# The second feed-forward product from fp32r parts, moved behind the projections in odd steps, with its sum behind the cosines

## Chip, cores and metric

One core of one Trainium2 chip. The metric is the device time of one execution in microseconds.

## What is computed

A small attention layer on x (2 x 2048 x 256, 16 heads of 16, full attention, in the reference `_L0_attn_ref`) is followed by two layers of local attention with a gated feed-forward part, with residual sums and normalisations between them. The change lies in the feed-forward part of these two layers:

```python
def _layer(x, wqkv, qs, ksc, wo, lg, lb, w1, b1, w2, b2):
    h = shift_token(x)
    q, k, v = jnp.split(h @ wqkv, 3, axis=-1)
    ...
    x = x + o @ wo
    h = shift_token(x)
    mu = h.mean(-1, keepdims=True)
    var = h.var(-1, keepdims=True)
    h = (h - mu) / jnp.sqrt(var + 1e-05) * lg + lb
    h = h @ w1 + b1
    a, g = jnp.split(h, 2, axis=-1)
    h = a * jax.nn.gelu(g, approximate=False)
    x = x + h @ w2 + b2
    return x
```

h has 682 columns before the last product, x has 256. `shift_token` takes half of the columns from the token before.

## The kernel before

The kernel has three phases. `project_phase` makes q, k and v of the first attention layer. `attention_phase` runs its 32 heads, one after another; beside them it splits the weights of the later phase into fp32r parts (a high part, rounded, and a low part, the rest), piece by piece: SyncE loads a piece (`prepare_weights`), GpSimd rounds and subtracts (`split_piece`), SyncE stores both parts in DRAM. `feed_forward_phase` does the rest; the change is there.

The feed-forward phase handles 64 tiles of 128 tokens (32 of each layer, the two batches in turn) in a software pipeline. Each engine has its own hand-written order, one round of `for t in steps`. In step t an engine works on tile t+3 (transposed x), t+2 (projections, rotary tables, norms), t+1 (local attention), t (normalisation) and on the pair of tiles behind it: in an even step the first product with w1 (`hidden`), GELU (`gelu`, ScalarE) and gate (`gated`, VectorE) of tiles t-2 and t-1; in an odd step the second product with w2 (`hidden_out`, TensorE) of tiles t-3 and t-2, and its sum onto x (`add_hidden`, VectorE). PSUM has eight banks that all these share; most of the waits at the head of a function are for a bank.

The order of an odd step on TensorE is: `scores`, `hidden_out` (line 1358) of tile t-3, `project` (line 1191: three products into three banks, each from fp32r parts), `transposed_probs` (1261), `transposed_hidden_in` (1237), `hidden_out` of tile t-2, `outputs_of_heads` (1303), `transposed_q_k` (1326), `attended` (1342), `transposed_x` (1175).

On VectorE: `mask_and_maximum` (1584) of tile t+1, `split_xT`, the sum `add_hidden` (1615) of tile t-3, `mean_and_variance` (1622) of tile t, which needs x shifted by one token (two DMAs between partitions, from `shift` on SyncE, after the residual sum `add_attended`, 1682, that closes the step before), `normalise` (1598), two `cosines` (1641), `normalise_mid` (1634), `copy_PT` (1655), `square_norms` (1649), `copy_PT`, `rotate` (1662), `scale_keys` (1669), `add_hidden` of tile t-2, `add_attended`.

ScalarE: `exponentials` (1427) of tile t+1, `copy_projected` (1438 to 1441: copy and square of q, copy and square of k, copy of v), `copy_PT` (1448), `affine` (1456), in even steps `gelu`, then `copy_oT`, `copy_qT_kT` (1481, 1483), `round_xT` (1488, 1490). GpSimd: `normalise` (1046), `inverse_deviation` (1051), `add_b2` (1056), `sines` (1067, two instructions; they wait for the copy of k, VectorE's cosines for the squares), `inverse_norms` (1074, 1076), `split_y`, every second step `rotary_tables`.

`hidden_out` takes the gated values `act_T` and w2 as fp32; the projections and `hidden` take fp32r parts, high x high, high x low and low x high, added up in one bank. The pairs of sums and waits that matter:

```python
def normalise_mid(v):
    dve.wait_ge(rstd_made, v + 1)
    if v:
        dve.wait_ge(hT_done, v)
```

Of the kernel before, what the change touches and what calls it, by code (L numbers as in the profile page):

```python
# [6 lines left out]
F32 = mybir.dt.float32  # L7
BF16 = mybir.dt.bfloat16
F32R = mybir.dt.float32r
# [4 lines left out]
P = 128  # L14
# [369 lines left out]
def attention_phase(nc, ins, division, VO, mask_sb, weights, ident, load_output_weights, stacks, qkT_stored):  # L384

    with ExitStack() as ctx:
# [3 lines left out]
        q_stack, k_stack, q_minus_first = stacks.q, stacks.k, stacks.q_minus  # L390
        v_ones = sb("v_ones", [P, BODY, TB, VW])
        probs = sb("probs", [P, PROBS, 512])
        excess = probs[:, PROBS - BLOCKS:].rearrange("p (i k) c -> p i k c", i=2)
        spare_pieces = weights.tables[:].rearrange("p a t h d -> p (a t h d)").rearrange("p (i c) -> p i c", c=PIECE)
        raw_piece, piece_hi, piece_lo = spare_pieces[:, 0], spare_pieces[:, 1].bitcast(F32R), spare_pieces[:, 2].bitcast(F32R)
# [61 lines left out]
        def _(sp):  # L457
# [33 lines left out]
            for n in range(NH):  # L491
# [16 lines left out]
                if n == TABLES_HEAD:  # L508
                    sp.wait_ge(weights.parts_stored, 32 * (len(PIECES) - IN_PLACE))
                    weights.load_tables(sp, ins)  # L510
# [9 lines left out]
        def _(pool):  # L520
# [23 lines left out]
            def split_piece(i):  # L544
# [3 lines left out]
                if i < IN_PLACE:  # L548
                    _, _, k, columns = PIECES[i]
                    hi, lo = weights.wqkv_hi[0][:, k, columns], weights.wqkv_lo[:, k, columns]  # L550
# [154 lines left out]
        def _(dve):  # L705
# [70 lines left out]
          + [("w1", l, k, slice(a, min(a + PIECE, W1_COLUMNS))) for l in range(LAYERS) for k in range(NC) for a in range(0, W1_COLUMNS, PIECE)])  # L776
# [3 lines left out]
class Weights:  # L780


    def __init__(self, nc, ctx, stacks):
# [5 lines left out]
        self.wqkv_hi = [sb("wqkv2_hi0", [P, NC, 3 * INNER], F32R)]  # L789
        self.wqkv_lo = sb("wqkv2_lo", [P, NC, 3 * INNER], F32R)  # L790
        self.tables = sb("tables2", [P, 2, TB, 2, D2 // 2])
# [8 lines left out]
        self.tables_loaded, self.small_loaded = sem("tables2_loaded"), sem("small2_loaded")  # L800
        self.wqkv1_loaded, self.w1_loaded, self.wo_loaded, self.w2_loaded = (sem(n) for n in ("wqkv2_1_loaded", "w1_2_loaded", "wo2_loaded", "w2_loaded"))

    def place_wide(self, ctx, stacks):
# [5 lines left out]
        self.w2 = sb("w2_sb", [P, HC, C])  # L809

    def place_second(self, in_k):

        self.wqkv_hi.append(in_k(NC, 3 * INNER))

    def raw_piece(self, ins, i):
        name, l, k, columns = PIECES[i]
        return ins[name][l].rearrange("(k p) n -> p k n", p=P)[:, k, columns]

    def stored_piece(self, i, part):
        name, l, k, columns = PIECES[i]  # L820
        return self.wqkv_parts[part, :, k, columns] if name == "wqkv2" else self.w1_parts[l, part, :, k, columns]

    def load_tables(self, eng, ins):
        for i, name in enumerate(("cos2", "sin2")):
            eng.dma_start(self.tables[:, i], ins[name].rearrange("(t p) (a d) -> p t a d", p=P, a=2)).then_inc(self.tables_loaded, 16)
# [18 lines left out]
    def load_w2(self, eng, ins, l):  # L844
        eng.dma_start(self.w2[:], ins["w2"][l].rearrange("(k p) n -> p k n", p=P)).then_inc(self.w2_loaded, 16)

    def load_first(self, eng, ins):
# [3 lines left out]
        self.load_w2(eng, ins, 0)  # L851

    def load_second_wqkv(self, eng, part):
        place = (self.wqkv_hi[1], self.wqkv_lo)[part]
        eng.dma_start(place[:].bitcast(F32), self.wqkv_parts[part]).then_inc(self.wqkv1_loaded, 16)


def feed_forward_phase(nc, ins, weights, stacks, division, x_sb, outputs, spare, wo1_loaded, x1_dram, mask_sb, ident, out):

    with ExitStack() as ctx:  # L860
# [17 lines left out]
        weights.place_second(in_k)  # L878
        wqkv_hi, wqkv_lo, (w1_hi, w1_lo), wo_sb, w2_sb = weights.wqkv_hi, weights.wqkv_lo, weights.w1, weights.wo, weights.w2
        qks_sb, cos_sb, sin_sb, b2_sb = weights.qk_scale, weights.tables[:, 0], weights.tables[:, 1], weights.b2  # L880
# [29 lines left out]
        act_T = gate  # L910
# [27 lines left out]
        x1_stored = [sem(f"x1_stored{i}") for i in range(3)]  # L938
        shifted, x1_loaded, out_stored = [sem(f"shifted{i}") for i in range(2)], [sem(f"x1_loaded{i}") for i in range(2)], sem("out_stored")
# [32 lines left out]
        def _(sp):  # L972
# [14 lines left out]
            def shift(v):  # L987
# [5 lines left out]
                if v < 2:  # L993
                    sp.wait_ge(columns_made, 3)
# [9 lines left out]
            weights.load_second_wqkv(sp, 0)  # L1004
            for t in steps:
                if t == 1:
# [895 lines left out]
```

## Time and profile before

| | |
|---|---|
| median of 3 runs | 2899.72 us (2899.66 to 2905.52) |
| the profiled execution | 2905.26 us, of which the span of its instructions is 2903.4 us |
| TensorE busy | 2807.7 us (97%) |
| VectorE busy | 2323.1 us (80%) |
| ScalarE busy | 2113.7 us (73%) |
| GpSimd busy | 960.1 us (33%) |
| second product, line 1358 | 768 records, 195.8 us |
| `normalise_mid`, line 1634 | 64 instructions, 32.7 us |

In the profile PE is TensorE's multiplications, PEld its loads of weights, DVE VectorE, ACT ScalarE, POOL GpSimd, SP SyncE. A share of busy time is a mean over three phases with different limits, so it says little on one step. Instructions of an engine overlap a little in the records: the next often starts some 0.08 to 0.1 us before the one before ends. Times within the span are in us from its start. The feed-forward phase takes the second half of the span; a pair of its steps repeats about every 40.4 us, and tiles 40 and 41 stand for it here. Bank names are left out in the rows, so many operations read `bank<-...`: the line tells them apart.

### The profile page before, as it was taken

To read this page: it belongs to the slowest core of one execution; us is meant where nothing else is said; L and a number is where in the kernel's file an instruction comes from. 1 tells how busy PE (TensorE), PEld (TensorE's weight loads), DVE (VectorE), ACT (ScalarE), POOL (GpSimd) and SP (SyncE) were. 2 spreads that over 40 slices of the span, in tenths; PEclk is the share of its full clock that TensorE was granted. 3 is DMA by queue.
4 is the path that set the end of the run, shared out by engine and by line. 5 is a ranking of instruction groups with operands and counts; after the bars stand their busy time and mean duration, and the time that the engine had idled before them with its cause. 6 is when DMAs were issued, how large, how long until landed. Compare 5 with 4: busy or idle time off the path is not lost. (4 is left out here: it accounts for less than half of the span.)

```text
span 2903.4 us, 59150 instructions
## 1 busy us (share of the span) xinstructions
PE 2807.7 (97%) x22608; PEld 1755.0 (60%) x22608; DVE 2323.1 (80%) x4287; ACT 2113.7 (73%) x4556; POOL 960.1 (33%) x1102
## 2 busy tenths in 40 slices
PE   7999999999999999999997899999999999999997
PEld 7743333333333333333355788888887788888886
DVE  7779999999999999999816677777776677777774
ACT  5568888888888888888856566666666676666763
POOL 7600000010001000000016555555555555656553
PEclk9869999999999999999998899999999999999999
DMA  5613334443444243424203000000000100000000
GB/s 164 189 18 53 52 46 60 62 72 59 70 61 72 55 68 60 74 43 66 42 22 128 11 5 4 5 5 4 5 4 34 54 12 19 19 19 11 20 18 25
DMA packets 85944, 131.33 MB, mean 45 GB/s; under 512 B 33120, under 2 KB 59168, under 8 KB 78240
## 3 DMA queue, kind: packets, MB, share of 16 engines
q1 hardware_dynamic: 79376, 120.41, 21.1%
q10 hardware_dynamic: 6288, 7.14, 0.8%
q8 instruction: 181, 2.97, 0.5%
q14 instruction: 99, 0.81, 0.1%
HBM read 83.98 MB, written 34.61 MB: 41 GB/s over the span
## 5 line engine op out<-in xcount | busy, mean ns | idle before, releaser
L684 ACT ACTIVATE probs<-scores 128x512 f32<-128x512 f32 x2048 | 1114.7, 596 | 199.2 <-PE scores L610 76.3
L717 DVE TENSOR_REDUCE mx<-aux 128x1 f32<-128x1024 f32 x982 | 1201.1, 1223 | 61.4 <-PE aux L578 54.1
L578 PE MATMUL aux<-k_stack,q_stack 48*128 48x512 f32 x2006 | 757.4, 453 | 6.4 <-DMA k_stack<-qk_dram 4.1
L610 PE MATMUL scores<-q_stack,k_stack 50*128 50x512 f32 x2048 | 762.5, 450 | 0.0
L623 PE MATMUL pv<-probs,v_ones 128*32 128x256 f32 x8192 | 658.5, 393 | 0.1
L610 PEld LDWEIGHTS scores<-q_stack,k_stack 50*128 50x128 f32 x2048 | 310.2, 186 | 428.8 <-ACT probs L684 411.2
L623 PEld LDWEIGHTS pv<-probs,v_ones 128*32 128x32 f32 x8192 | 161.7, 108 | 361.5 <-ACT probs L684 289.4
L578 PEld LDWEIGHTS aux<-k_stack,q_stack 48*128 48x128 f32 x2006 | 306.4, 188 | 38.0 <-DVE mx L717 19.2
L531 POOL CAST m_parts<-head_max 128x16 fp32r<-128x16 f32 x32 | 6.3, 198 | 938.6 <-DVE head_max L710 938.6
L1427 ACT ACTIVATE VO<-VO,tables_small 128x256 f32<-128x256 f32 (+1 forms) x512 | 250.9, 492 | 48.7 <-DVE tables_small L1584 48.5
L1289 PE MATMUL bank<-q_minus_first,q_stack 128*128 128x256 f32 x2112 | 268.5, 285 | 0.6 <-DVE x_sb L1615 0.6
L1289 PEld LDWEIGHTS bank<-q_minus_first,q_stack 128*128 128x128 f32 x2112 | 256.5, 191 | 11.0 <-issue 10.9
L1584 DVE CUSTOM_DVE_ANT_0 VO<-bank,mask_sb,tables_small 128x256 f32<-128x256 f32 (+1 forms) x512 | 216.1, 469 | 52.0 <-PE bank L1222 52.0
L1046 POOL TENSOR_TENSOR VO<-VO,tables_small 128x512 f32<-128x512 f32 (+1 forms) x128 | 127.3, 1015 | 347.9 <-DVE tables_small L1592 347.9
L1067 POOL TENSOR_TENSOR VO<-VO,tables_small 128x512 f32<-128x512 f32 x128 | 166.1, 1319 | 99.2 <-issue 99.2
L1358 PE MATMUL bank<-w_sb,gate 128*128 128x256 f32 (+1 forms) x768 | 195.8, 397 | 1.3 <-DVE gate L1676 1.1
L1076 POOL TENSOR_TENSOR tables_small<-tables_small 128x16 f32<-128x16 f32 x64 | 189.6, 2962 | 5.3
L1358 PEld LDWEIGHTS bank<-w_sb,gate 128*128 128x128 f32 (+1 forms) x768 | 137.6, 192 | 47.4 <-issue 31.7
L1191 PE MATMUL bank<-wqkv_lo,k_stack 128*128 128x512 f32 x384 | 152.2, 396 | 0.0
L1476 ACT COPY oT<-bank 128x512 f32<-128x512 f32 x64 | 37.6, 587 | 155.5 <-PE bank L1303 155.5
L1438 ACT COPY VO<-bank 128x512 f32<-128x512 f32 x128 | 75.1, 587 | 83.9 <-PE bank L1191 83.9
L1191 PE MATMUL bank<-wqkv_hi,k_stack 128*128 128x512 f32 x384 | 128.6, 402 | 5.2 <-DVE tables_small L1584 2.7
(173 smaller groups left out, 4334.9 us busy)
## 6 DMA issues: line engine op xcount, KB each, us to landing
q_stack<-qk_dram SPq DMA_DIRECT2D x192, 128.0 KB, 5.1
k_stack<-qk_dram SPq DMA_DIRECT2D x192, 128.0 KB, 7.2
qk_dram<-qkT_hi SPq DMA_DIRECT2D x32, 256.0 KB, 3.7
qk_dram<-qkT_lo SPq DMA_DIRECT2D x32, 256.0 KB, 3.8
VO<-o_stage SPq DMA_DIRECT2D x128, 32.0 KB, 6.9
q_minus_first<-sums_dram SPq DMA_DIRECT2D x32, 128.0 KB, 2.9
w_parts<-tables SPq DMA_DIRECT2D x16, 256.0 KB, 2.5
x_dram<-x_sb SPq DMA_DIRECT2D x16, 256.0 KB, 2.0
```

The source lines that it names most:

```text
L578: return nc.tensor.matmul(out, q_stack[max_rows, n % BODY, tile * P:(tile + 1) * P], k_stack[max_rows, n % BODY, keys * 512:(keys + 1) * 512],
L610: last = nc.tensor.matmul(out, k_stack[0:SCORE_ROWS, n % BODY, s * P:(s + 1) * P], q_stack[0:SCORE_ROWS, n % BODY, j * 512:(j + 1) * 512], ...
L623: last = nc.tensor.matmul(pv[VW * j:VW * (j + 1), columns], v_ones[:, n % BODY, s, :], probs[:, (BLOCKS * step + j) % PROBS, columns], sta ...
L684: nc.scalar.activation(probs[:, e % PROBS], scores[:, item_of_exp(e) % BANKS1], ACT.Exp, scale=float(D1) ** -0.5).then_inc(act_emptied, 1)
L717: nc.vector.tensor_reduce(mx[:, n % BODY, tile, half:half + 1], aux[:, unit % 2].rearrange("p a k -> p (a k)"), AX.X, ALU.max).then_inc(dv ...
L1067: last = nc.gpsimd.tensor_tensor(out=o4[:, :, :, lo:lo + D2 // 2], in0=q4[:, :, :, hi:hi + D2 // 2], in1=sin_table[:, v // 2 % 2, :, lo:lo ...
L1076: nc.gpsimd.tensor_tensor(out=rnorm[:, v % 2], in0=norm2_min, in1=minus_half, op=ALU.pow).then_inc(rnorm_made, 1)
L1191: last = nc.tensor.matmul(bank[QKV_BANK[a]][:], x_part[:, v % 4, k, tokens], w_part[:, k, columns], start=(k == 0 and n == 0), stop=(k == ...
L1289: last = nc.tensor.matmul(out_half, w_part[:, k, chunk * P:(chunk + 1) * P], h_part[:, p % 2, k], start=(k == 0 and n == 0), stop=(k == NC ...
L1358: last = nc.tensor.matmul(bank[F_BANK[v % 2]][:, 0:C], act_T[rows, c, v % 2 * P:(v % 2 + 1) * P], w2_sb[rows, c], start=(c == 0), stop=(c ...
L1427: last = nc.scalar.activation(probs[j][:, u, keys], probs[j][:, u, keys], ACT.Exp, scale=-1.0, bias=negmax[:, j, u:u + 1], accum_out=sums[ ...
L1584: last = nc.vector.tensor_tensor_reduce(out=probs[j][:, u, at:at + n_keys], in0=src[:, 2 * u * P + at:2 * u * P + at + n_keys], in1=mask_s ...
```

## The change

- `hidden_out` takes fp32r parts: 18 multiplications (three groups of 6 chunks) in place of 6 in fp32. Its waits are now for the parts.
- ScalarE rounds the gated values into `act_hi` in two instructions of 128x768 (`round_hidden`), around `round_xT` of each even step. GpSimd subtracts them into `act_lo` in two of 128x768 (`split_hidden`), behind `split_y` of each even step. `gelu` of the next pair now waits for the subtraction.
- In odd steps TensorE runs `project` before `hidden_out(t - 3)`, and VectorE runs `add_hidden(t - 3)` behind the two cosines, directly before `normalise_mid`.
- w2 is split into parts in the attention phase (6 more pieces), and both parts are loaded (1.5 MB per layer in place of 768 KB).
- To make room, the tables of cosines and sines are loaded per pair of tiles, by SyncE in odd steps (two loads of 32 KB), and not all at once; and wqkv of the second layer has one place, loaded by ScalarE's queue in one go before step 30, and not half at the start by SyncE's.

```diff
@@ hidden_out
                 if v % NT == 0:
-                    pe.wait_ge(weights.w2_loaded, 16 * (layer(v) + 1))
-                pe.wait_ge(act_made, HC * (v // 2 + 1))
+                    pe.wait_ge(weights.w2_loaded, 32 * (layer(v) + 1))
...
-                for c in range(HC):
-                    rows = slice(0, P if c < HW else HR)
-                    last = nc.tensor.matmul(bank[F_BANK[v % 2]][:, 0:C], act_T[rows, c, v % 2 * P:(v % 2 + 1) * P], w2_sb[rows, c], start=(c == 0), stop=(c == HC - 1))
+                out, tokens = bank[F_BANK[v % 2]][:, 0:C], slice(v % 2 * P, (v % 2 + 1) * P)
+                for i, (a_part, w_part) in enumerate(((act_hi, w2_hi), (act_hi, w2_lo), (act_lo, w2_hi))):
+                    for c in range(HC):
+                        if c % (HC // 2) == 0 and i != 1:
+                            pe.wait_ge(act_high_made if i == 0 else act_split, 2 * (v // 2) + c // (HC // 2) + 1)
+                        rows = slice(0, P if c < HW else HR)
+                        last = nc.tensor.matmul(out, a_part[rows, c, tokens], w_part[rows, c], start=(i == 0 and c == 0), stop=(i == 2 and c == HC - 1))
                 last.then_inc(F_done, 1)
@@ TensorE's steps
+                if exists(t + 2):
+                    project(t + 2)
                 if t % 2 == 1 and exists(t - 3):
                     hidden_out(t - 3)
-                if exists(t + 2):
-                    project(t + 2)
@@ ScalarE
                     if j == 0 and p:
-                        act.wait_ge(F_done, 2 * p)
+                        act.wait_ge(act_split, 2 * p)
...
+            def round_hidden(p, i):
+
+                chunks = slice(i * HC // 2, (i + 1) * HC // 2)
+                act.wait_ge(act_made, HC * p + chunks.stop)
+                if i == 0 and p:
+                    act.wait_ge(F_done, 2 * p)
+                nc.scalar.copy(act_hi[:, chunks], gate[:, chunks]).then_inc(act_high_made, 1)
...
+                if t % 2 == 0 and exists(t - 2):
+                    round_hidden((t - 2) // 2, 0)
                 if t >= 0 and exists(t + 3):
                     round_xT(t + 3)
+                if t % 2 == 0 and exists(t - 2):
+                    round_hidden((t - 2) // 2, 1)
@@ GpSimd
+            def split_hidden(p):
+
+                for i in range(2):
+                    chunks = slice(i * HC // 2, (i + 1) * HC // 2)
+                    pool.wait_ge(act_high_made, 2 * p + i + 1)
+                    nc.gpsimd.tensor_tensor(out=act_lo[:, chunks], in0=gate[:, chunks], in1=act_hi[:, chunks], op=ALU.subtract).then_inc(act_split, 1)
@@ VectorE's steps
-                if not even and exists(t - 3):
-                    add_hidden(t - 3)
                 if exists(t):
                     mean_and_variance(t)
...
+                if not even and exists(t - 3):
+                    add_hidden(t - 3)
                 if exists(t):
                     normalise_mid(t)
@@ SyncE's steps
+                if t % 2 == 1 and exists(t + 5):
+                    p = (t + 5) // 2
+                    sp.wait_ge(tables_made, 2 * (p - 1))
+                    weights.load_tables(sp, ins, p)
```

Three places of the instruction streams. On TensorE in an odd step (L1358 is the second product before and L1376 now; L1191 and L1206 are the projections), first before, then now:

```order
L1222 MATMUL bank<-VO,qT 128x256 x8
L1358 MATMUL bank<-w_sb,gate 128x256 x6
...
L1191 MATMUL bank<-wqkv_lo,k_stack 128x512
L1191 MATMUL bank<-wqkv_hi,k_stack 128x512
L1261 MATMUL bank<-ident,VO 128x128 x16
L1237 MATMUL bank<-ident,wo_bo_sb 128x128 x2
L1358 MATMUL bank<-w_sb,gate 128x256 x6
L1303 MATMUL bank<-PT,VO 64x128 x16
L1326 MATMUL bank<-ident,VO 128x128 x8
```

```order
L1237 MATMUL bank<-VO,qT 128x256 x8
...
L1206 MATMUL bank<-wqkv_lo,k_stack 128x512
L1206 MATMUL bank<-wqkv_hi,k_stack 128x512
L1376 MATMUL bank<-w_hi,k_stack 128x256 x6
L1376 MATMUL bank<-w_lo,k_stack 128x256 x6
L1376 MATMUL bank<-w_hi,k_stack 128x256 x6
L1276 MATMUL bank<-ident,VO 128x128 x16
L1252 MATMUL bank<-ident,wo_bo_sb 128x128 x2
L1376 MATMUL bank<-w_hi,k_stack 128x256 x6
L1376 MATMUL bank<-w_lo,k_stack 128x256 x6
L1376 MATMUL bank<-w_hi,k_stack 128x256 x6
L1318 MATMUL bank<-PT,VO 64x128 x16
```

The first product of the step stands behind the projections, and each of the two is three groups of six.

On VectorE in an odd step, from the last reciprocal of the maxima on, first before, then now (L1615 and L1645 are `add_hidden`, L1641 and L1671 the cosines, L1634 and L1664 `normalise_mid`):

```order
L1592 RECIPROCAL tables_small<-tables_small 128x2
L1615 TENSOR_TENSOR x_sb<-bank,x_sb 128x256
L1622 BN_STATS tables_small<-x_mid 128x6 x2
L1625 BN_AGGR tables_small<-tables_small 128x2
L1627 TENSOR_SCALAR tables_small<-tables_small 128x1
L1592 RECIPROCAL tables_small<-tables_small 128x2
L1598 TENSOR_TENSOR VO<-VO,tables_small 128x512
L1592 RECIPROCAL tables_small<-tables_small 128x2
L1598 TENSOR_TENSOR VO<-VO,tables_small 128x512
L1641 TENSOR_TENSOR VO<-bank,tables_small 128x512 x2
L1634 TENSOR_SCALAR wo_bo_sb<-x_mid,tables_small 128x256
```

```order
L1622 RECIPROCAL tables_small<-tables_small 128x2
L1652 BN_STATS tables_small<-x_mid 128x6 x2
L1655 BN_AGGR tables_small<-tables_small 128x2
L1657 TENSOR_SCALAR tables_small<-tables_small 128x1
L1622 RECIPROCAL tables_small<-tables_small 128x2
L1628 TENSOR_TENSOR VO<-VO,tables_small 128x512
L1622 RECIPROCAL tables_small<-tables_small 128x2
L1628 TENSOR_TENSOR VO<-VO,tables_small 128x512
L1671 TENSOR_TENSOR VO<-bank,tables_small 128x512 x2
L1645 TENSOR_TENSOR x_sb<-bank,x_sb 128x256
L1664 TENSOR_SCALAR wo_bo_sb<-x_mid,tables_small 128x256
```

The sum has moved from in front of the statistics to between cosines and `normalise_mid`.

On ScalarE at the end of an even step, now (L1497 is `round_hidden`, L1514 and L1516 `round_xT`, L1445 the exponentials of the odd step):

```order
L1502 COPY oT<-bank 128x512
L1507 COPY qT<-bank 128x512
L1509 COPY VO<-bank 128x512
L1497 CAST k_stack<-gate 128x768
L1514 CAST k_stack<-bank 128x2x128
L1516 CAST k_stack<-bank 128x1
L1497 CAST k_stack<-gate 128x768
L1445 ACT_TABLE_LOAD
L1445 ACTIVATE VO,tables_small<-VO,tables_small 128x256 x8
```

The two roundings are new; the second stands before the table load of the exponentials.

## Rows read from the trace of the kernel before

**Rows 1.** Busy times by stretch, even and odd step: length, busy time of each engine, granted clock, DMA.

```profile
2403.67:2424.69 21.02, 21.02 (x170) 18.98 (x168) 15.61 (x45) 15.51 (x40) 11.82 (x11) 1.00 0.09 29
2424.69:2444.07 19.38, 18.99 (x128) 15.27 (x126) 14.79 (x46) 12.12 (x32) 12.36 (x14) 1.00 0.01 4
```

**Rows 2.** TensorE's timeline, odd step: start, length, instructions, idle time before them.

```profile
2440.79 1.09 PE L1326 MATMUL bank<-ident,VO 128*128 128x128 f32 x8 [0.39 <-DVE VO L1669]
```

**Rows 3.** Chain that ended last, both steps: start, length, what ran.

```profile
2405.36 4.49 PE bank L1289 x36
...
2426.38 2.98 PE bank L1358 x12
2429.36 4.38 PE bank L1191 x18
...
2436.89 2.95 POOL tables_small L1076
```

**Rows 4.** VectorE's timeline, both steps.

```profile
2408.62 0.49 DVE L1622 BATCH_NORM_STATS2 tables_small<-x_mid 128x6 f32<-128x128 f32 x2 [0.23 <-DMA x_mid<-x_mid]
...
2420.94 1.25 DVE L1676 SCALAR_TENSOR_TENSOR gate<-bank,b_dve,gate 128x256 f32<-128x256 f32 x3
...
2429.40 0.42 DVE L1615 TENSOR_TENSOR x_sb<-bank,x_sb 128x256 f32<-128x256 f32 x1
2429.74 0.48 DVE L1622 BATCH_NORM_STATS2 tables_small<-x_mid 128x6 f32<-128x128 f32 x2
...
2433.51 0.69 DVE L1641 TENSOR_TENSOR VO<-bank,tables_small 128x512 f32<-128x512 f32 x1 [0.30 <-ACT VO L1439]
2434.11 0.44 DVE L1634 TENSOR_SCALAR wo_bo_sb<-x_mid,tables_small 128x256 f32<-128x256 f32 x1
2434.65 0.69 DVE L1655 COPY PT<-bank 128x512 f32<-128x512 f32 x1
```

**Rows 5.** ScalarE's timeline, end of the even step and odd step.

```profile
2422.59 0.59 ACT L1483 COPY VO<-bank 128x512 f32<-128x512 f32 x1
2424.49 0.37 ACT L1488 CAST k_stack<-bank 128x256 fp32r<-128x256 f32 x1 [1.31 <-PE bank L1175]
2424.76 0.17 ACT L1490 CAST k_stack<-bank 128x1 fp32r<-128x1 f32 x1
2424.94 1.28 ACT L1427 ACT_TABLE_LOAD   x1
2426.48 0.51 ACT L1427 ACTIVATE VO<-VO,tables_small 128x256 f32<-128x256 f32 x1 [0.26 <-DVE tables_small L1584]
...
2430.39 0.18 ACT L1427 ACTIVATION_READ_ACCUMULATOR VO<-VO,tables_small 128x1 f32 x1
...
2432.38 0.59 ACT L1438 COPY VO<-bank 128x512 f32<-128x512 f32 x1 [0.30 <-PE bank L1191]
2432.87 0.61 ACT L1439 ACTIVATE VO<-bank 128x512 f32<-128x512 f32 x1
```

**Rows 6.** GpSimd's subtractions of weight pieces: busy, mean ns, idle before.

```profile
L558 POOL TENSOR_TENSOR tables<-tables 128x512 fp32r<-128x512 f32 x14 | 18.0, 1286 | 1.1
```

**Rows 7.** GpSimd's timeline, odd step.

```profile
2428.62 2.04 POOL L1046 TENSOR_TENSOR VO<-VO,tables_small 128x512 f32<-128x512 f32 x2 [7.01 <-DVE tables_small L1592]
...
2433.11 1.29 POOL L1067 TENSOR_TENSOR VO<-VO,tables_small 128x512 f32<-128x512 f32 x1 [1.05 <-issue]
2434.36 1.33 POOL L1067 TENSOR_TENSOR VO<-VO,tables_small 128x512 f32<-128x512 f32 x1
```

**Rows 8.** Timelines of GpSimd and VectorE at tile 33.

```profile
2269.49 1.27 POOL L1067 TENSOR_TENSOR VO<-VO,tables_small 128x512 f32<-128x512 f32 x1
...
2269.53 1.39 DVE L1634 TENSOR_SCALAR wo_bo_sb<-x_mid,tables_small 128x256 f32<-128x256 f32 x1
```

**Rows 9.** All of line 1634: shortest, median and longest in ns.

```profile
L1634 DVE TENSOR_SCALAR wo_bo_sb<-x_mid,tables_small x64: 402/430/1394, 1596.5 to 2872.2; 128x256 f32<-128x256 f32 x64
```

**Rows 10.** Chain that ended last, tile 34.

```profile
2280.95 7.65 DMA x_mid<-x_mid
```

More of the change, by code:

```diff
@@ L508, in _ @@
                 if n == TABLES_HEAD:
-                    sp.wait_ge(weights.parts_stored, 32 * (len(PIECES) - IN_PLACE))
-                    weights.load_tables(sp, ins)
+                    for p in range(2):
+                        weights.load_tables(sp, ins, p)
                 if n == TABLES_HEAD + 1:
@@ L549, in split_piece @@
                     _, _, k, columns = PIECES[i]
-                    hi, lo = weights.wqkv_hi[0][:, k, columns], weights.wqkv_lo[:, k, columns]
+                    hi, lo = weights.wqkv_hi[:, k, columns], weights.wqkv_lo[:, k, columns]
                 else:
@@ L842, in load_w1, with load_w2 @@
             eng.dma_start(self.w1[part].bitcast(F32), self.w1_parts[l, part]).then_inc(self.w1_loaded, 16)
-    def load_w2(self, eng, ins, l):
-        eng.dma_start(self.w2[:], ins["w2"][l].rearrange("(k p) n -> p k n", p=P)).then_inc(self.w2_loaded, 16)
+    def load_w2(self, eng, l):
+        for part in range(2):
+            eng.dma_start(self.w2[part][:].rearrange("p k n -> p (k n)").bitcast(F32), self.w2_parts[l, part]).then_inc(self.w2_loaded, 16)
     def load_first(self, eng, ins):
@@ L850, in load_first, with load_second_wqkv @@
         self.load_w1(eng, 0)
[L851 to L855, printed above, removed]
+        self.load_w2(eng, 0)
+    def load_second_wqkv(self, eng):
+        for part, place in enumerate((self.wqkv_hi, self.wqkv_lo)):
+            eng.dma_start(place[:].bitcast(F32), self.wqkv_parts[part]).then_inc(self.wqkv1_loaded, 16)
 def feed_forward_phase(nc, ins, weights, stacks, division, x_sb, outputs, spare, wo1_loaded, x1_dram, mask_sb, ident, out):
@@ L1675, in gated @@
                 rows, column = (slice(0, P), j) if j < HW else (slice(0, HR), 2 * HW)
-                nc.vector.scalar_tensor_tensor(act_T[rows, j], bank[H_BANK[j]][rows, 0:2 * P], b1_dve[rows, layer(2 * p), column:column + 1],
+                nc.vector.scalar_tensor_tensor(gate[rows, j], bank[H_BANK[j]][rows, 0:2 * P], b1_dve[rows, layer(2 * p), column:column + 1],
                                                gate[rows, j], ALU.add, ALU.mult).then_inc(act_made, 1)
```

58 lines of the change are left out of this document (32 added, 26 removed).

## The prediction

> **What bounds the kernel now.** I read the busy shares by stage first, then the chain that ended last, then each engine's timeline over one pair of steps of the second half. The second half (the feed-forward phase, tiles 0 to 63) repeats a pair of steps: an even one of 21.02 us and an odd one of 19.38 us, at a granted clock of 1.00 [rows 1]. In the even step TensorE is busy for 21.02 of 21.02 us: it is the bound. In the odd step it is busy for 18.99 us and idle for 0.39 us, all of it before the transposes of q and k, which wait for VectorE's `scale_keys` [rows 2]. So two things run level in an odd step: TensorE's own work, and a chain through the other engines. The chain of waits shows that second one: after the projections it leaves TensorE, goes over VectorE's reduction to `inverse_norms` on GpSimd (2.95 us) and `scale_keys` on VectorE, and returns to TensorE at 2440.79 [rows 2, 3]. What TensorE saves in an odd step is therefore worth only what that chain gives back too.
>
> Before the reduction the chain is one row of instructions on VectorE. In the odd step they are: the sum `add_hidden` at 2429.40, statistics at 2429.74, second cosine product at 2433.51 (after 0.30 us of waiting for ScalarE's square), `normalise_mid` at 2434.11, copy of the probabilities at 2434.65 [rows 4]. The square comes from ScalarE's copies of the projections, and these wait for TensorE: 0.30 us before the second one [rows 5].
>
> **The product itself.** Now 12 records in 2.98 us (TensorE takes each fp32 multiplication as two) [rows 3]. The same shape from fp32r parts runs 36 in 4.49 us, 0.125 us each [rows 3], so 18 cost 2.25 us. TensorE saves 0.73 us a tile, 1.46 us a pair, 47 us over 32 pairs: that is the ceiling of the gain. All of it lies in odd steps, where TensorE would then be idle for 0.39 + 1.46 = 1.85 us unless the chain gets shorter.
>
> **Rounding on ScalarE.** Two copies of 128x768 per even step. A copy of 512 columns takes 0.59 us, one of 256 takes 0.37 us [rows 5], so 768 take 0.81 us. The first starts when the copies of q and k end at 2423.18, in the 1.31 us of idle time before the next instruction [rows 5]: free. The second stands between the rounding of xT (ends 2424.93) and the table load at 2424.94. The exponentials of the odd step waited 0.26 us more for VectorE, from 2426.22 to 2426.48 [rows 5]; so they start at about 2427.0, and are 0.5 us later. They end at 2431.1 instead of 2430.57.
>
> **Subtraction on GpSimd.** Two of 128x768 per even step. 512 columns of this form took 1.29 us [rows 6]; 768 take 1.9 us at most. Started at 2424.0 and 2425.9 they end at 2427.8, inside the idle time that lasts until 2428.62 [rows 7]. VectorE's work in that stretch reads PSUM with one tile of SBUF, and TensorE wants the parts only at about 2430.7. Free.
>
> **Projections in front of the product.** They no longer wait for the first product's 2.98 us; the maxima that free their banks hold them a little. Three of them take 4.38 us [rows 3], so from 2426.4 on the second one is done by about 2429.3, and ScalarE, free at 2431.0, no longer waits for TensorE. Call c the start of its second copy: first copy at 2431.0, square 0.49 us later, second copy again 0.5 us later, c = 2432.0; before, c was 2432.38 [rows 5]. So the cosines gain 0.38 us at ScalarE's end, in spite of the later exponentials.
>
> **The sum behind the cosines.** In front of the statistics it was free but for 0.1 us: they need the shifted rows anyway, which land 4.95 us after the residual sum that opens a step (even step: from 2403.67 [rows 1] to 2408.62 [rows 4]); in the odd step that gives 2429.64 against a start at 2429.74. Behind the cosines it costs its 0.34 us (2429.40 to 2429.74) on the chain. Taken alone, 0.38 less at c and 0.34 more is nothing. But what comes next is a tie between VectorE and GpSimd.
>
> `normalise_mid` reads and writes SBUF, while GpSimd runs the two halves of `sines`, 1.25 us from start to start. Before, they started at 2433.11 and 2434.36, and `normalise_mid` was issued at 2434.11, ahead of the second half: it got in between and ended at 2434.55 [rows 4, 7]. At tile 33 it came at 2269.53, 0.04 us after the second half (2269.49), and took 1.39 us: until that half was over [rows 8]. The longest of all 64 is 1.394 us, the median 0.430 [rows 9]. So whichever is issued first goes first, and the loser waits for a whole instruction.
>
> Who is first now? Written from c: GpSimd starts 0.73 after c (2433.11 against 2432.38), its second half at c + 1.98. The square starts 0.49 after c and takes 0.61; the cosine follows 0.03 later, at c + 1.13, and is followed 0.60 later. Before, that was `normalise_mid` at c + 1.73, 0.25 ahead. Now the sum stands between and makes it c + 2.07: **0.09 us too late**, whatever c is, since both sides hang on ScalarE. The second half then ends at c + 3.25 (1.27 us, as at tile 33 [rows 8]) and the copy behind `normalise_mid` starts at about c + 3.33 = 2435.33 instead of 2434.65 [rows 4]. The chain is 0.68 us longer. The Trainium skill has this as a rule (page "SBUF — State Buffer", section "Who interferes with whom"): a `tensor_scalar` in its two-port mode and a GpSimd instruction share a pair of ports, and whichever issues first holds it for its whole length. By it the change pays these 0.68 us, and without it the sum would be that of the first rival below; the trace agrees, at tiles 33 and 41.
>
> **Waits and queues.** ScalarE's roundings wait for VectorE's gate products (the last ends at 2422.19 [rows 4]) and for the second product of the pair before; behind them stand only the xT rounding and the exponentials, priced above. GELU now waits for the subtraction, over long before the next pair's GELU. TensorE's product waits for both parts, ready 3 us before. On SyncE two loads of 32 KB each stand in odd steps behind that step's shift of rows and long before the next; GpSimd uses them a pair later. Where the shift did share the engines with a store and a load of 256 KB (tile 40) it still landed after 4.95 us [rows 4].
>
> **The sum.** The sum and the cosines meet in steps 3 to 61, 30 of them; in steps 31 and 33 `normalise_mid` was late already, which leaves 28. 28 x 0.68 = 19 us. Once only: the weights of the second layer. Behind the load of 768 KB for the second product the shifted rows took 7.65 us instead of about 4.9 [rows 10]; it is twice as large now, so up to 2.8 us more. At the end the last two products save 0.7 us each, less the rounding and subtraction that nothing covers there: about -1. Tables of 64 KB per pair, six more pieces split in the attention phase (on GpSimd, which is mostly idle there) and the load of wqkv in one piece: nothing, if the shifted rows land on time; between -2 and +4 together. Sum: +19 + 2 = +21 us. The profiled execution took 2905.3 us, so it would take 2926; the median of the runs is 2899.7, near the lower of two levels, and the prediction is made for that: **2921 us**. If this case holds, 2910 to 2930.
>
> **Rivals.**
> - *The lock is won.* 0.09 us is a narrow margin, made of five pitches that are read to 0.01 us each. If the sum or the cosine is quicker by that much, or GpSimd wakes later, `normalise_mid` goes in between again and the copy behind it starts near c + 2.35 = 2434.35, 0.30 us earlier than now. 28 x -0.30 + 2 = -6: 2893 us; with everything a little better, 2885. This is the other side: faster. For it: it lost by only 0.04 us at tile 33. Against it: the same 0.04 us was enough to lose.
> - *TensorE's saving counts in full.* The odd steps get shorter by 1.46 us: 2853 us. It needs a chain through VectorE that is 1.46 us shorter, and I find no row that gives more than 0.4.
> - *Half way.* The wait is real, but slack takes some of it, or the gain at c is smaller: within 0.2% of now.
> - *Much slower.* Rounding or subtraction take longer than their slots (0.5 us and 0.8 us), or the table loads hold the shifted rows back; each 0.1 us on the odd chain is 3 us. Above 2931 us.
>
> **How the numbers follow.** Lost lock 0.56, won lock 0.23, half way 0.11, full saving 0.04, much slower 0.06. About 0.2% (5.8 us) is what a measurement of this kernel can tell from no change. Slower by more than that: the lost lock and the last rival with a small part of "half way", 0.64. Within it: 0.11. Faster: won lock and full saving, most of it, 0.25. As cases of both signs count, the range takes both in: 2886 (won lock) to 2931.
>
> **What would show it.** In the profile after: `normalise_mid` near 1.3 us in the odd steps and 0.43 us in the even ones; its mean near 0.9 us instead of 0.51; odd steps of about 20.1 us, even ones still 21.0; TensorE idle for about 2.5 us before the transposes of q and k in odd steps; the second product at 2.2 us a tile; ScalarE no longer waiting before its second copy. I am wrong if `normalise_mid` stays at 0.43 us, if even steps change their length, or if the odd steps come near 18 us.

## The result, and the profile after

The changed kernel took 2953.3 us (median of 4 runs, 2952.2 to 2955.0) against 2899.9 us before (4 runs, 2899.7 to 2905.5): a ratio of 1.0183, with a 95% interval of 1.0167 to 1.0199. It is slower, as forecast, but by 53 us and not by 21, and the time lies outside the range.

The busy times of the two stretches that answer to [rows 1]:

```profile
2430.63:2451.67 21.04, 21.04 (x170) 19.00 (x168) 15.60 (x45) 16.34 (x41) 12.40 (x12) 1.00 0.10 30
2451.67:2472.68 21.01, 19.56 (x140) 16.00 (x138) 14.77 (x45) 12.54 (x33) 15.30 (x16) 1.00 0.03 7
```

The even step is as long as before. The odd step is 21.01 us and not 19.38, at the same granted clock of 1.00. TensorE is busy for 0.57 us more of it, where it should have saved 1.46 us, and idle for 1.45 us.

TensorE's timeline in that odd step, with [rows 2 and 3] beside it:

```profile
2454.68 0.50 PE L1206 MATMUL bank<-wqkv_hi,k_stack 128*128 128x512 f32 x1 [1.33 <-DVE k_stack L1638]
...
2458.97 1.06 PE L1376 MATMUL bank<-w_hi,k_stack 128*128 128x256 f32 x6
2459.95 1.15 PE L1376 MATMUL bank<-w_lo,k_stack 128*128 128x256 f32 x6
2461.03 1.15 PE L1376 MATMUL bank<-w_hi,k_stack 128*128 128x256 f32 x6
2462.12 1.97 PE L1276 MATMUL bank<-ident,VO 128*128 128x128 f32 x16
```

Two things are new. The projections (L1206) wait 1.33 us for VectorE's line 1638, the split of xT. And the product (L1376) runs from 2458.97 to 2462.12: 3.15 us, not 2.25. The transposes of the probabilities (L1276) stand behind it.

VectorE's timeline of the same step, with [rows 4]:

```profile
2454.14 0.42 DVE L1633 TENSOR_TENSOR k_stack<-bank,k_stack 128x256 fp32r<-128x256 f32 x1
2454.48 0.15 DVE L1638 TENSOR_TENSOR k_stack<-bank,k_stack 128x1 fp32r<-128x1 f32 x1
...
2456.62 0.49 DVE L1652 BATCH_NORM_STATS2 tables_small<-x_mid 128x6 f32<-128x128 f32 x2 [0.23 <-DMA x_mid<-x_mid]
...
2459.42 1.27 DVE L1671 TENSOR_TENSOR VO<-bank,tables_small 128x512 f32<-128x512 f32 x2
2462.22 0.42 DVE L1645 TENSOR_TENSOR x_sb<-bank,x_sb 128x256 f32<-128x256 f32 x1 [1.52 <-PE bank L1376]
2462.56 0.41 DVE L1664 TENSOR_SCALAR wo_bo_sb<-x_mid,tables_small 128x256 f32<-128x256 f32 x1
2463.25 0.69 DVE L1685 COPY PT<-bank 128x512 f32<-128x512 f32 x1 [0.28 <-PE bank L1276]
```

The sum (L1645) does not cost its 0.34 us. It waits 1.52 us for the product, and `normalise_mid` (L1664) and the copy stand behind it. `normalise_mid` takes 0.41 us: the second half of the sines was over by then (GpSimd, next rows). The statistics still start 4.95 us after the residual sum, so the transfers arrive as before.

GpSimd's and ScalarE's timelines, with [rows 5 and 7]:

```profile
2451.09 3.59 POOL L1099 TENSOR_TENSOR k_stack<-gate,k_stack 128x768 fp32r<-128x768 f32 x2 [2.51 <-ACT k_stack L1497]
...
2459.56 2.52 POOL L1073 TENSOR_TENSOR VO<-VO,tables_small 128x512 f32<-128x512 f32 x2 [0.61 <-issue]
```

```profile
2450.18 0.83 ACT L1497 CAST k_stack<-gate 128x768 fp32r<-128x768 f32 x1
...
2451.78 0.85 ACT L1497 CAST k_stack<-gate 128x768 fp32r<-128x768 f32 x1
2452.65 1.28 ACT L1445 ACT_TABLE_LOAD   x1
2453.94 0.51 ACT L1445 ACTIVATE VO<-VO,tables_small 128x256 f32<-128x256 f32 x1
...
2458.85 0.57 ACT L1456 COPY VO<-bank 128x512 f32<-128x512 f32 x1
```

Rounding and subtraction sit where they were expected, and ScalarE's second copy (L1456, 2458.85) no longer waits.

**Where the 49.8 us between the two profiled executions lie** (spans 2953.2 and 2903.4), from the ends of the 64 residual sums (`add_attended`): 28 odd steps at +1.62 us are +45.3; the step to tile 35 is +3.2; what follows tile 63 is +4.9; the first residual sum ends 2.5 us earlier; the rest of the steps together are -1.1.

### The profile page after: what moved, and what is told of

The parts are those of the page before. It is cut to its first block, busy times and chain, and to the rows that moved or that the text cites. A ratio compares the mean times of both kernels' runs of the same rounds, so it can differ in the third digit from the quotient of the medians.

```text
span 2953.2 us, 60204 instructions
## 1 busy us (share of the span) xinstructions
PE 2823.0 (96%) x22992; PEld 1778.0 (60%) x22992; DVE 2322.7 (79%) x4287; ACT 2154.0 (73%) x4620; POOL 1085.0 (37%) x1179
## 3 DMA queue, kind: packets, MB, share of 16 engines
q8 instruction: 184, 3.01, 0.5%
## 4 chain that ended last, share of the span: by engine, by line
PE 35%; DVE 6%; POOL 5%; issue 2%; DMA 1%; ACT 1%; SPq 0%; POOLq 0%; DVEq 0%; ACTq 0%
PE bank L1206 8%; PE bank L1304 8%; PE bank L1357 4%; POOL tables_small L1082 4%; PE bank L1376 3%; PE bank L1237 3%; PE bank L1276 3%; PE bank L1341 2%; PE bank L1318 2%; DVE VO L1614 2%; DVE tables_small L1679 1%; DVE VO L1699 1%; DMA x_mid<-x_mid 1%; DMA x_mid<-q_minus_first 1%; PE bank L1393 0%
## 5 line engine op out<-in xcount | busy, mean ns | idle before, releaser
L1206 PE MATMUL bank<-wqkv_hi,k_stack 128*128 128x512 f32 x768 | 255.8, 401 | 46.4 <-DVE k_stack L1638 39.6
L1445 ACT ACTIVATE VO<-VO,tables_small 128x256 f32<-128x256 f32 (+1 forms) x512 | 250.6, 491 | 41.7 <-DVE tables_small L1614 41.3
L1206 PEld LDWEIGHTS bank<-wqkv_hi,k_stack 128*128 128x128 f32 x768 | 145.1, 189 | 90.9 <-DVE k_stack L1638 51.3
L1206 PE MATMUL bank<-wqkv_lo,k_stack 128*128 128x512 f32 x384 | 152.1, 396 | 0.0
L1376 PE MATMUL bank<-w_hi,k_stack 128*128 128x256 f32 (+1 forms) x768 | 146.8, 311 | 2.3 <-ACT k_stack L1497 1.4
L1099 POOL TENSOR_TENSOR k_stack<-gate,k_stack 128x768 fp32r<-128x768 f32 x64 | 115.4, 1827 | 89.7 <-ACT k_stack L1497 89.7
```

What stands on the lines that cost most here:

```text
L1206: last = nc.tensor.matmul(bank[QKV_BANK[a]][:], x_part[:, v % 4, k, tokens], w_part[:, k, columns], start=(k == 0 and n == 0), stop=(k == ...
L1376: last = nc.tensor.matmul(out, a_part[rows, c, tokens], w_part[rows, c], start=(i == 0 and c == 0), stop=(i == 2 and c == HC - 1))
L1445: last = nc.scalar.activation(probs[j][:, u, keys], probs[j][:, u, keys], ACT.Exp, scale=-1.0, bias=negmax[:, j, u:u + 1], accum_out=sums[ ...
```

## Experiments

All of them are compared by the odd step from tile 41 to 42. Times in it are counted from its opening, the end of the residual sum of tile 41 (2424.69 before, 2451.67 after), and called offsets. Its length is the firmer measure: the start of the phase alone moved by up to 19 us from one profiled execution to the next, while the odd steps of one execution agree within 0.15 us, apart from steps 1, 31 and 33 and at most two more. The even step was 21.02 to 21.04 us in every run.

**Move without the parts.** The kernel before, with only its order changed on TensorE and VectorE; the product stays fp32.

```diff
-                if t % 2 == 1 and exists(t - 3):
-                    hidden_out(t - 3)
                 if exists(t + 2):
                     project(t + 2)
+                if t % 2 == 1 and exists(t - 3):
+                    hidden_out(t - 3)
...
-                if not even and exists(t - 3):
-                    add_hidden(t - 3)
                 if exists(t):
                     mean_and_variance(t)
...
+                if not even and exists(t - 3):
+                    add_hidden(t - 3)
                 if exists(t):
                     normalise_mid(t)
```

> The kernel before with the move alone: projections ahead of the first second product and its sum behind the cosines, product still fp32. Theory A, the move itself exposes the wait for the low part of x (1.3 us) and makes the sum wait for the product: odd steps of 20.7 to 21.0 us, about 2940 us. Rival B, the move is harmless and the parts are at fault: within 5 us of 2900.

Measured: 2944.1 us, ratio 1.0146 (1.0129 to 1.0163); odd step 20.75 us. TensorE's timeline of it:

```profile
2454.17 0.50 PE L1191 MATMUL bank<-k_stack 128*128 128x512 f32 x1 [1.33 <-DVE k_stack L1608]
...
2458.46 2.95 PE L1358 MATMUL bank<-w_sb,gate 128*128 128x256 f32 x12
```

Theory A holds. The move brings 1.37 of the 1.63 us by itself, and the same wait of 1.33 us in front of the projections. In the order before, the first product stood there and covered it.

**Parts without the move.** The changed kernel, with the order of before on both engines.

```diff
+                if t % 2 == 1 and exists(t - 3):
+                    hidden_out(t - 3)
                 if exists(t + 2):
                     project(t + 2)
-                if t % 2 == 1 and exists(t - 3):
-                    hidden_out(t - 3)
...
+                if not even and exists(t - 3):
+                    add_hidden(t - 3)
                 if exists(t):
                     mean_and_variance(t)
...
-                if not even and exists(t - 3):
-                    add_hidden(t - 3)
                 if exists(t):
                     normalise_mid(t)
```

> Changed kernel in the kernel before's order: the second product from fp32r parts, but in front of the projections on TensorE, and its sum in front of the statistics on VectorE. Theory A (the loss is the move's, and the product, at 3.15 us for 2.98, saves nothing): odd step 19.4 to 19.7 us, total 2900 to 2910 us. Rival B (the parts cost by themselves: rounding on ScalarE, subtraction on GpSimd, loads of tables): odd step over 20.3 us, above 2925 us.

Measured: 2919.0 us, ratio 1.0049 (1.0036 to 1.0063); odd step 19.69 us. The step came out as theory A said, the total 9 us above its bound. Beside the steps it has the late transfer at tile 35 (+2.3 us) and the long end (+5.1 us) of the changed kernel, and the kernel before, run beside it, had a median of 2905.8 us, 6 us more than in the result above. The parts by themselves, with 64 rows in the last chunk, save nothing.

**All 128 rows in the sixth chunk.** The sixth chunk has 64 rows of values. The rest of it holds zeros in both factors, so the sum is the same with all rows.

```diff
-                        rows = slice(0, P if c < HW else HR)
+                        rows = slice(0, P)
```

> The changed kernel, but the sixth chunk of the second product is multiplied over all 128 rows (its rows beyond 64 are zeros in both operands, so the result is the same). Theory A, the product is dear because it goes from a 128-row chunk to the 64-row one and back three times: each product takes 18 x 0.118 = 2.1 us instead of 3.1, the sum behind the cosines stops waiting for it by as much, odd steps get 1.0 us shorter, about 2925 us. Rival B, it is dear because each multiplication loads other weights than the one before: still 3.1 us and 2953 us.

Measured: 2916.4 us, ratio 1.0062 (1.0040 to 1.0084); odd step 19.92 us. The product on TensorE:

```profile
2434.00 0.86 PE L1376 MATMUL bank<-w_hi,k_stack 128*128 128x256 f32 x6
2434.70 0.87 PE L1376 MATMUL bank<-w_lo,k_stack 128*128 128x256 f32 x6
2435.41 0.87 PE L1376 MATMUL bank<-w_hi,k_stack 128*128 128x256 f32 x6
2436.12 1.91 PE L1276 MATMUL bank<-ident,VO 128*128 128x128 f32 x16
```

It now takes 2.12 us (2434.00 to 2436.12) in place of 3.15. More rows made it a third shorter. Theory A holds: the odd step is 1.09 us shorter. The total is 9 us under its 2925. In the profiled executions the end, behind tile 63, is 4.8 us shorter than in the changed kernel, which theory A had not counted, and the first residual sum ends 6 us earlier, which is within the spread of that start. In the changed kernel the records are, grouped by shape:

```profile
L1376 PE MATMUL bank<-w_hi,k_stack 128*128 128x256 f32 x640 | 106.6, 296 | 2.3 <-ACT k_stack L1497 1.4 <-POOL k_stack L1099 0.6 <-DVE PT L1685 0.2
...
L1376 PE MATMUL bank<-w_hi,k_stack 64*128 64x256 f32 x128 | 49.3, 385 | 0.0
```

The one with half the rows is the longer one. The kernel before has such a visit too, one per product: at tile 41 its records start 0.216 us apart, but 0.31 us apart into the 64-row chunk, 0.32 inside it and 0.31 behind it. How much its fp32 product would gain from full rows was not run.

**Is it the change of the row count, or something in the parts?** The two loops of the product exchanged, still with 64 rows in the last chunk.

```diff
-                for i, (a_part, w_part) in enumerate(((act_hi, w2_hi), (act_hi, w2_lo), (act_lo, w2_hi))):
-                    for c in range(HC):
+                for c in range(HC):
+                    for i, (a_part, w_part) in enumerate(((act_hi, w2_hi), (act_hi, w2_lo), (act_lo, w2_hi))):
```

> Changed kernel with the two loops of the second product exchanged: for each of the six chunks the three products of parts follow each other, so that TensorE goes to the chunk with 64 rows and back once per tile and not three times. Same instructions, same rows, same count. Theory A (what makes the product 3.15 us long and not 2.25 is the change of the number of rows, some 0.3 us for each visit to the 64-row chunk): about 2.5 us a tile, odd step about 20.3 us, total about 2935 us. Rival B (it is the change of weights between the parts, or the parts' place in SBUF): stays at 3.1 us or gets longer, odd step 21.0 us, 2953 us.

Measured: 2933.9 us, ratio 1.0098 (1.0075 to 1.0122); odd step 20.20 us. Start and end of the product:

```profile
2444.48 0.28 PE L1376 MATMUL bank<-w_hi,k_stack 128*128 128x256 f32 x1
...
2446.13 0.59 PE L1376 MATMUL bank<-w_hi,k_stack 128*128 128x256 f32 x2
2446.56 0.28 PE L1376 MATMUL bank<-w_lo,k_stack 64*128 64x256 f32 x1
2446.68 0.27 PE L1376 MATMUL bank<-w_hi,k_stack 64*128 64x256 f32 x1
2446.88 1.97 PE L1276 MATMUL bank<-ident,VO 128*128 128x128 f32 x16
```

2.40 us. One visit to the chunk with 64 rows costs 0.28 us more than none (2.40 against 2.12), three cost 1.03 us (3.15): 0.28 to 0.34 us a visit. Inside the visit, multiplications follow each other at 0.12 us (2446.56, 2446.68). Theory A holds. The rival with the change of parts or their place falls with the run before this one, which left order, parts and places alone and changed only the rows. What in TensorE makes the visit cost this is not shown.

**The split in front of the maxima.** In odd steps VectorE splits xT before the first two maxima.

```diff
                 even, finished = t % 2 == 0, finished_pair(t)
+                if not even and t >= 0 and exists(t + 2):
+                    split_xT(t + 2)
                 if exists(t + 1):
                     mask_and_maximum(t + 1, 0)
                     mask_and_maximum(t + 1, 1)
-                if t >= 0 and exists(t + 2):
+                if even and exists(t + 2):
                     split_xT(t + 2)
```

> The changed kernel, but in odd steps VectorE makes the low part of the transposed x in front of the first two maxima and not behind them. Theory A, TensorE's 1.33 us in front of the projections is a wait for this instruction alone: it shrinks to 0.1 us, odd steps get 1.1 to 1.3 us shorter, about 2920 us. Rival B, the projections would wait for the maxima that free their banks, or ScalarE's exponentials and copies bound the step anyway: the wait gets another name and the time stays within 5 us of 2953.

Measured: 2929.3 us, ratio 1.0098 (1.0078 to 1.0119); odd step 19.89 us, with 0.21 us of waiting before the projections in place of 1.33. VectorE's timeline:

```profile
2452.89 0.42 DVE L1645 TENSOR_TENSOR x_sb<-bank,x_sb 128x256 f32<-128x256 f32 x1 [0.41 <-PE bank L1376]
2453.23 0.81 DVE L1664 TENSOR_SCALAR wo_bo_sb<-x_mid,tables_small 128x256 f32<-128x256 f32 x1
```

The step came out as theory A said, the total 9 us above its 2920. The sum's wait is down to 0.41 us, and `normalise_mid` is up to 0.81. What is left of the wait before the projections ends with the maxima (line 1614).

**Both together.** Full rows and the split first.

> Both edits: all 128 rows, and the low part first. Theory A1, the product leaves the path and the lock that the prediction told of comes forward: normalise_mid is issued 0.1 us behind GpSimd's second half of sines, takes 1.3 us in the odd steps, and the time is near that of the better edit alone, 2918 to 2924 us. Theory A2, no lock: the two gains add up, odd steps of 19.0 us, about 2897 us.

Measured: 2922.5 us, ratio 1.0076 (1.0051 to 1.0101); odd step 19.89 us. It is no shorter than with either alone. VectorE and, below it, GpSimd:

```profile
2438.14 1.28 DVE L1671 TENSOR_TENSOR VO<-bank,tables_small 128x512 f32<-128x512 f32 x2
2439.34 0.41 DVE L1645 TENSOR_TENSOR x_sb<-bank,x_sb 128x256 f32<-128x256 f32 x1
2439.67 1.29 DVE L1664 TENSOR_SCALAR wo_bo_sb<-x_mid,tables_small 128x256 f32<-128x256 f32 x1
2440.88 0.68 DVE L1685 COPY PT<-bank 128x512 f32<-128x512 f32 x1
```

```profile
2438.28 2.52 POOL L1073 TENSOR_TENSOR VO<-VO,tables_small 128x512 f32<-128x512 f32 x2 [0.62 <-issue]
```

This is the step that the forecast described: the sum waits for nothing, `normalise_mid` is issued after the second half of the sines and takes 1.29 us. It is theory A1. In the runs with full rows, with the split first and with both it started at offsets of 9.96, 9.75 and 9.27 us, took 0.61, 0.81 and 1.29 us, and ended at 10.57, 10.56 and 10.56, always 0.15 us behind GpSimd (10.41).

**The sum behind the rotation.** The last kernel, with the sum moved on, so that `normalise_mid` follows the cosines directly.

```diff
-                if not even and exists(t - 3):
-                    add_hidden(t - 3)
                 if exists(t):
                     normalise_mid(t)
...
                 if exists(t + 2):
                     rotate(t + 2)
+                if not even and exists(t - 3):
+                    add_hidden(t - 3)
```

> Changed kernel with all 128 rows in every chunk, the split of xT in front of the maxima in odd steps, and the sum moved on, from behind the cosines to behind the rotation. Theory A (with the two waits of TensorE gone, the odd step hangs on the race of normalise_mid with the second half of the sines; without the sum ahead of it normalise_mid is issued first): normalise_mid 0.43 us in odd steps where it took 1.28, odd step about 19.0 us instead of 19.9, total about 2895 us, level with the kernel before or a little below. Rival B (the race costs nothing, the odd step hangs on the path over inverse_norms and scale_keys in any case): odd step 19.7 to 19.9, about 2918 us.

Measured: 2886.6 us (2883.4 to 2890.1), ratio 0.9933 (0.9914 to 0.9953): faster than both kernels. Odd step 18.70 us. VectorE:

```profile
2425.04 1.28 DVE L1671 TENSOR_TENSOR VO<-bank,tables_small 128x512 f32<-128x512 f32 x2
2426.24 0.40 DVE L1664 TENSOR_SCALAR wo_bo_sb<-x_mid,tables_small 128x256 f32<-128x256 f32 x1
2426.56 0.69 DVE L1685 COPY PT<-bank 128x512 f32<-128x512 f32 x1
```

`normalise_mid` is issued in time and takes 0.40 us; the copy starts at an offset of 9.28 us in place of 10.48. Step and total are both a little better than theory A had them. Lost race and sum together were worth 1.2 us of each odd step.

**Only the sum moved.** The same edit on the changed kernel, without the other two.

> Changed kernel with one thing moved: the sum of the second product stands behind the rotation and not behind the cosines. Theory A (the first copy of the probabilities waits for its transposes, which stand behind the product on TensorE, so the sum's wait of 1.52 us only hides that one): normalise_mid comes early, the copy still starts 11.6 us into the odd step, waits some 1.9 us for TensorE, and the odd step stays at 21.0 us, total 2950 to 2955 us. Rival B (the sum's place on VectorE is what costs): the wait goes with it, odd step 19.4 us or less, total 2905 us or below.

Measured: 2955.4 us, ratio 1.0166 (1.0129 to 1.0204); odd step 21.01 us. VectorE:

```profile
2473.18 0.40 DVE L1664 TENSOR_SCALAR wo_bo_sb<-x_mid,tables_small 128x256 f32<-128x256 f32 x1
2475.82 0.69 DVE L1685 COPY PT<-bank 128x512 f32<-128x512 f32 x1 [2.24 <-PE bank L1276]
```

Nothing is gained. With the sum out of the way `normalise_mid` is done 2 us earlier, and the copy waits 2.24 us for the transposes, which stand behind the product on TensorE. The sum's wait of 1.52 us only lay on top of that one.

**Sum moved and full rows,** with the split behind the maxima as in the changed kernel.

> The same with all 128 rows in every chunk (so the run with the sum behind the rotation, but with the split of xT left behind the first two maxima). Theory A: the transposes of the probabilities start 9.4 us into the odd step, 1.0 us earlier than in the changed kernel, and the copy waits for them: it starts at about 10.5 us, normalise_mid takes 0.40 us, odd step 19.9 to 20.0 us, total about 2917 us. Rival B (with the race out of the way the wait of the projections for the split is harmless): odd step 18.8 us as with the split first, total about 2887 us.

Measured: 2922.5 us, ratio 1.0062 (1.0041 to 1.0084); odd step 19.91 us. VectorE:

```profile
2445.90 0.69 DVE L1685 COPY PT<-bank 128x512 f32<-128x512 f32 x1 [1.14 <-PE bank L1276]
```

No race, no sum, and yet 19.91 us: now it is TensorE's row alone, with its 1.33 us in front of the projections. Theory A holds in both runs, with this total 5 us above its 2917.

**Parts in the old order, with full rows.** The edit of the rows on the run with the parts in the old order.

> As the run with the parts in the old order, but with all 128 rows in every chunk, so that the product takes about 2.2 us. Theory A: the odd step follows the product where the product stands in front of the projections, so 0.3 to 0.8 us less than the kernel before: about 19.0 us, total 2885 to 2895 us, faster than both kernels. Rival B (the chain over inverse_norms is what the odd step hangs on already): odd step 19.4, 2900 us.

Measured: 2890.3 us (7 runs, 2882.4 to 2900.0), ratio 0.9946 (0.9923 to 0.9970): the second version that beats both kernels. Odd step 18.68 us, 0.3 us better than theory A had it. With full rows the parts do save time, 0.70 us of each odd step. As fp32 with full rows was not run, how much of that is the rows' alone is open.

**All steps in one table.** Offsets in us, all worked out from the timelines of the odd step from tile 41 to 42. "Transposes" is the start of `transposed_probs` on TensorE, "norm." the end of `normalise_mid`, "copy" the start of VectorE's first copy of the probabilities. "Both" is full rows and the split first.

| kernel | transposes | norm. | copy | step | step less copy |
|---|---|---|---|---|---|
| before | 8.88 | 9.86 | 9.96 | 19.38 | 9.42 |
| changed | 10.45 | 11.30 | 11.58 | 21.01 | 9.43 |
| move alone | 10.19 | 11.04 | 11.32 | 20.75 | 9.43 |
| parts, old order | 9.19 | 10.15 | 10.26 | 19.69 | 9.43 |
| loops exchanged | 9.65 | 10.55 | 10.78 | 20.20 | 9.42 |
| full rows | 9.42 | 10.57 | 10.49 | 19.92 | 9.43 |
| split first | 9.30 | 10.56 | 10.48 | 19.89 | 9.41 |
| both | 8.27 | 10.56 | 10.48 | 19.89 | 9.41 |
| sum moved alone | 10.45 | 9.35 | 11.58 | 21.01 | 9.43 |
| sum moved, full rows | 9.41 | 9.35 | 10.49 | 19.91 | 9.42 |
| sum moved, both | 8.20 | 9.35 | 9.28 | 18.70 | 9.42 |
| parts, old order, full rows | 8.02 | 9.35 | 9.27 | 18.68 | 9.41 |

In all twelve the step ends 9.41 to 9.43 us after the copy starts. And the copy starts at the later of two times: 1.07 to 1.13 us after the transposes start on TensorE, or 0.08 us before `normalise_mid` ends on VectorE. Each row can be checked against that.

## Why the prediction came out as it did

- **Projections in front of the product: here it failed.** The prediction let them start at 2426.4, an offset of 1.7 us, and said that the maxima "hold them a little". They started at 3.01. What holds them is the split of xT, which stands on VectorE behind the first two maxima. Before, the projections started at 4.60, behind the product's 2.98 us, and never met it. VectorE's timeline of the kernel before had the row, and it ends at the same offset of 2.96 us as in the changed kernel:

```profile
2427.51 0.14 DVE L1608 TENSOR_TENSOR k_stack<-bank,k_stack 128x1 fp32r<-128x1 f32 x1
```

The run with the split first takes 1.12 us of the wait away, and the step is 1.12 us shorter. There the projections start at 1.90 and only the maxima hold them: with the split out of the way the forecast of 1.7 was nearly right.
- **The product itself: mis-sized.** 3.15 us measured for 2.25. The pitch of 0.125 us came from [rows 3], from a product without a chunk of fewer rows; for 128 rows it was nearly right (2.12 us for 18, 0.118 each). The three visits to the 64-row chunk cost 1.03 us. So TensorE saved nothing: the ceiling of 47 us was not there.
- **What this did to the sum.** Forecast: product done at 1.7 + 4.4 + 2.25 = 8.3 us, sum reached at c + 1.73, 9.0 us: a margin of 0.7 us that was not written down. Measured: product done at 10.45, sum reached at 9.03 us. The margin was overrun by 1.3 us in front and 0.9 us in the product, and the wait is 1.52 us.
- **The chain was read too narrowly.** "Before the reduction the chain is one row of instructions on VectorE" is wrong already for the kernel before, though by little. Its copy starts 1.08 us behind the transposes on TensorE (eight other rows of the table have 1.07 to 1.13), and 0.10 us after `normalise_mid` ends, where it could have started 0.08 us before that:

```profile
2433.58 1.91 PE L1261 MATMUL bank<-ident,VO 128*128 128x128 f32 x16
```

So TensorE's row led VectorE's by 0.18 us before, and the prediction counted nothing for it. With the change the transposes stand behind the late projections and the long product. That row then decides, whatever VectorE does; the run with only the sum moved shows it. The gap of 0.1 us before 2434.65 in [rows 4] was the sign.
- **The lock race: right, and not reached.** In the changed kernel `normalise_mid` comes at an offset of 10.89 us, after the sines (10.41), and takes 0.41 us. Where the two waits are gone it takes 1.29 us, the step 19.89 us (forecast: about 20.1) and the kernel 2922.5 us (forecast: 2921). The prediction's sum describes that kernel, but that the totals come within 2 us is in part luck: its odd steps are 0.51 us longer than before and not 0.68, so the 28 of them give 14 us and not 19. That the changed kernel moved the way that was forecast is luck too: the race, which was to make it slower, cost it nothing. The rule that the prediction took from the Trainium skill (page "SBUF — State Buffer", section "Who interferes with whom"), that whoever issues first holds the pair of ports for its whole length, fits the three runs in which `normalise_mid` ended at 10.56 to 10.57 us from three different starts.
- **Rounding and subtraction: right.** 0.83 and 0.85 us for 0.81; 1.83 us on average for at most 1.9. The exponentials start 0.48 us later for 0.5. ScalarE's second copy comes at an offset of 7.18 us: 7.31 forecast, 7.69 before.
- **Once only.** The shifted rows behind the load of the second layer's weights took 9.61 us for the 7.65 of [rows 10], and that step is 3.2 us longer (forecast: up to 2.8); the transfer gives 2.0 of it, the rest was not followed. The end is 4.9 us longer and not 1 shorter. There the granted clock of TensorE was at half for longer (two groups of rows below). Busy times in stretches of 4 us from the last residual sum on, in the columns of [rows 1], after:

```profile
2910.60:2914.60 4.00, 2.83 (x14) 1.90 (x13) 0.00 (x0) 0.00 (x0) 2.03 (x2) 1.00 0.05 15
2914.60:2918.60 4.00, 0.65 (x3) 0.66 (x4) 2.68 (x9) 0.00 (x0) 1.25 (x2) 0.61 0.01 2
2918.60:2922.60 4.00, 4.00 (x15) 3.10 (x14) 0.24 (x2) 0.81 (x2) 2.05 (x4) 0.50 0.00 0
2922.60:2926.60 4.00, 3.39 (x14) 2.90 (x14) 0.49 (x2) 1.09 (x2) 0.91 (x1) 0.50 0.00 0
2926.60:2930.60 4.00, 4.00 (x26) 4.00 (x25) 0.84 (x2) 0.95 (x2) 0.37 (x1) 0.68 0.44 135
```

and before, the same from the second stretch on:

```profile
2869.70:2873.70 4.00, 0.65 (x3) 0.65 (x4) 2.32 (x8) 0.00 (x0) 1.24 (x2) 0.61 0.01 2
2873.70:2877.70 4.00, 4.00 (x12) 2.88 (x10) 0.24 (x2) 0.81 (x2) 2.04 (x4) 0.54 0.00 0
2877.70:2881.70 4.00, 3.39 (x26) 3.02 (x26) 0.98 (x3) 1.57 (x3) 1.30 (x1) 1.00 0.01 4
```

In both, TensorE is busy for only 0.65 us in a stretch of 4 us, and with it the granted clock falls to about half (1.2 GHz). Before, it is back at 1.00 in the second stretch after that one; after the change it stays at 0.50 for two more and is 0.68 in the third. The runs on record tell where the long end belongs: what follows tile 63 is 4.8 to 5.4 us longer than before in all five kernels with parts and 64 rows in the last chunk, and between 0.7 us shorter and 1.8 us longer in the five with all 128 rows. How much of it is the clock and how much the product itself was not separated.
- **The rivals.** "TensorE's saving counts in full" fell for the reason given. "Much slower" had the size, but with other causes than late parts or late tables: both arrived in time.

## What to carry to other kernels

When an operation is moved out of a place, ask what it covered there: the next operation on that engine meets every wait that the old one used to sit out. Where an instruction waits for another engine, write down two times, when its own engine reaches it and when the other engine releases it, and take the later; a chain read from one engine's row hides the one that runs level with it. And take the price of a matrix product from rows with the same sequence of row counts, not from the same shape of output alone.

## What the runs showed of the hardware

- Going from a multiplication with 128 rows to one with 64 and back cost TensorE about 0.3 us a visit (fp32r, 256 columns). With 128 rows throughout they followed each other at 0.118 us (0.113 in the run with the sum behind the rotation). So padding the last chunk with zero rows made the product 1.03 us shorter, and grouping the 64-row multiplications brought 0.75 us of it.
- A `tensor_scalar` of VectorE that was issued while a GpSimd `tensor_tensor` ran ended 0.15 us after it, whether it had been issued 0.30, 0.45, 0.66 or 1.14 us before GpSimd's end (loops exchanged, full rows, split first, both). Alone it took 0.40 us.
